# A twelve-stage transformer stack on one core: gate products taken batch by batch and weighed on GpSimd, six copies of parts in place of seven, the first half of the stacks fetched alone, and the mixtures' small arrays awaited later

## The chip, the core and the metric

The kernel runs on 1 core of one Trainium2 chip, in one launch. The metric is the device time in microseconds (us). Five engines work beside each other and meet only at semaphores: TensorE (PE, matmuls into the eight PSUM banks), VectorE (DVE), ScalarE (ACT), GpSimd (POOL) and SyncE (SP, which here only issues DMAs). ACT issues a few DMAs too, and POOL issues the indirect ones.

## What is computed

`x` is 4 x 512 x 128 float32: 4 batches of 512 tokens (16 tiles of 128 tokens) with 128 channels. Twelve sublayers are added to it one after the other, each on a layer-normed `x`:

```python
x = x + 0.5 * ffn0(ln(x));  x = x + gla(ln(x));            x = x + 0.5 * ffn0(ln(x))
x = x + 0.5 * moe1(ln(x));  x = x + attention1(ln(x));     x = x + 0.5 * moe1(ln(x))
x = x + 0.5 * moe2(ln(x));  x = x + diff_attention2(ln(x)); x = x + 0.5 * moe2(ln(x))
x = x + 0.5 * ffn3(ln(x));  x = x + diff_attention3(ln(x)); x = x + 0.5 * ffn3(ln(x))
```

Three kinds of sublayer matter here. The gated linear attention (`gla`) takes, beside q, k and v, three gates per head:

```python
h = x * rsqrt(mean(x * x) + 1e-06) * norm_w
def gate(W, b):                       # for Wbeta, Wig, Wog; 8 heads each, 24 columns in all
    return sigmoid(einsum('bld,hd->blh', h, W) + b)
```

The first mixture (`moe1`) sends each token to one of 8 experts, the second (`moe2`) to two:

```python
logits = einsum('bsh,he->bse', x, router_w) + router_b          # moe1
expert_idx = argmax(logits, axis=-1)
h = gelu(einsum('bsh,hi->bsi', x + 0.1 * game_emb[e], w1[e]) + b1[e])
y = einsum('bsi,ih->bsh', h, w2[e]) + b2[e]                      # of the token's expert e
```

The attentions take scores between heads of 8 or 4 channels (`attention1`: `softmax(y y^T / sqrt(8))`, 16 heads; the differential ones: two softmaxes per head, one subtracted from the other).

## The kernel before, in words

Each stage is one or two blocks. In a block every engine runs its own list of instructions; a new block begins on all engines once all have ended the last. The order on each engine is the order of the code; waits on semaphores are written out by hand. All tensors of tokens lie as 128 partitions x 16 tiles x 128.

**Norm.** `norm_rows` (L355 on) has DVE write the normed rows `N`, one TENSOR_SCALAR for each tile (L362): four of batch 0, then three of each later batch, whose last row ACT writes (L377). `norm_turn` has PE transpose the four tiles of a batch into one PSUM bank (L398), and ACT copies the bank to `nT` (L383, `norm_take`).

**The head of `gla`.** PE transposes all four batches into banks 0 to 3. Then it waits for `weighted` and takes 16 gate products `nT x WA[:, 384:408]` (L618, 128 x 24 each, every float32 matmul shown as two passes) into bank 0. `weighted` comes from DVE, which multiplies the 128 x 408 weights by `norm_w` (L655) behind its rows, three memsets (L649 to L651) and a cast of `FUT` (L653). POOL only casts `HR` (L607, L608). From the gates there is one chain over DVE, ACT and PE (L660 to L684) to the end of the block.

**The head of a mixture.** The router's products are already in a bank when the stage begins. SP issues the small arrays (L1117: `fixed`, `UPTO`; in `moe1` then `rbias`, `b1`, `b2` of 1 MB and `game`), then the stores of the normed rows, then the down weights (L1150), and after `EIDI` is known the first up weights (L1158). DVE scales the logits (L1348), waits for all small arrays (`dve.wait_ge(small.sem, ...)`, in front of L1352), adds the router's bias (`moe1`), finds the chosen expert (`best_of`, L1338 to L1342, twice in `moe2`) and scans them (L1360). `fixed` is first read at L1366 (COLS). POOL waits for the same small arrays and makes `UPTOB` (L1175), for which, and for the scan, PE's products of ranks wait (L1247 to L1249). Their result starts a long DVE chain (L1372 on) to the row numbers `ROWS`, with which POOL gathers the tokens of the first expert (L1180).

**The head of an attention.** A projection is split into three bfloat16 parts (high by ACT, mid by ACT, low by POOL) held in `PART`. SP copies them into `scratch` in HBM, where each side (0 for q, 1 for k) has six slots; `copies` says which part goes to which slots, one DMA for each entry (L1841 and L2341). Scores contract over the slots, so that slot n of q meets slot n of k. When all is written, stacks `QS` and `KM` or `KS` are fetched in two halves (h = 0, 1), for batch 0 the k side by ACT's queue (L2051, L2468), the rest by SP's (L1860, L2350). In the differential attentions half 1 of batch 0 waits for half 0 already; in `attention1` it does not. PE's first score waits for half 0.

## Time and profile before

| | |
|---|---|
| median of 3 runs | 1893.79 us (1889.36 to 1898.24) |
| the profiled execution | 1894.98 us, span of its engines 1893.2 us |
| PE busy | 1501.6 us (79%) |
| DVE busy | 1083.7 us (57%) |
| ACT busy | 938.9 us (50%) |
| POOL busy | 372.6 us (20%) |
| mean granted TensorE clock | 0.888 of full speed |

The busy shares are means over twelve stages with different limits. The places of this change are short stretches at the heads of stages, in which one engine after the other waits; there the order of time and the waits are read, not the shares. Granted clock 0.50 is 1.2 GHz, 1.00 is 2.4 GHz. The time outside the span is 1.8 us.

### The profile page before, as it was taken

The numbers are of one execution on the slowest core, as the hardware profiler recorded it, in microseconds if no ns is written. First come the engines' busy times: TensorE is split into PE (matmuls) and PEld (weight loads), VectorE is DVE, ScalarE is ACT, GpSimd is POOL, SyncE is SP. The second block draws the span as 40 slices with busy tenths as digits, with TensorE's granted clock in tenths as the row PEclk, the third lists the DMA queues.
The fourth block names the chain that finished last, engine by engine and source line by source line (L and its number), as shares of the span: only waits on it lengthen the run. The fifth ranks groups of instructions, "written<-read, shape, count | busy, mean of one in ns | idle before, by whom it ended". The sixth has DMA issues, their size and how long they took to land. (4 is left out here: it accounts for less than half of the span.)

```text
span 1893.2 us, 27972 instructions
## 1 busy us (share of the span) xinstructions
PE 1501.6 (79%) x9134; PEld 815.3 (43%) x9134; DVE 1083.7 (57%) x2375; ACT 938.9 (50%) x2167; POOL 372.6 (20%) x538
## 2 busy tenths in 40 slices
PE   4895757999999495883899999994883958999768
PEld 4354643555555383872222222223773532222345
DVE  6575431333334526215988898957214758878466
ACT  3454334445444253223687878783222236777522
POOL 0230530000000171771311010000671001110000
PEclk7796777999999796996899999996896978999979
DMA  2002534020200455554121111003453023330000
GB/s 71 5 1 62 172 116 114 5 67 1 67 1 1 127 153 170 158 140 116 44 58 43 37 44 35 1 1 101 136 151 119 0 77 88 78 79 1 1 1 22
DMA packets 96046, 126.01 MB, mean 67 GB/s; under 512 B 14612, under 2 KB 65684, under 8 KB 95404
## 3 DMA queue, kind: packets, MB, share of 16 engines
q1 hardware_dynamic: 86252, 105.19, 19.5%
q0 software_dynamic: 7936, 16.27, 3.3%
q10 hardware_dynamic: 1728, 2.88, 0.8%
q8 instruction: 74, 1.21, 0.3%
q14 instruction: 56, 0.46, 0.1%
HBM read 87.49 MB, written 36.80 MB: 66 GB/s over the span
## 5 line engine op out<-in xcount | busy, mean ns | idle before, releaser
L2090 DVE TENSOR_REDUCE MAXI<-psum 128x2 f32<-128x1024 f32 x384 | 457.0, 1219 | 91.2 <-PE psum L1897 88.6
L2007 ACT ACTIVATE EX<-psum 128x512 f32<-128x512 f32 x768 | 412.6, 605 | 107.0 <-PE psum L1918 106.9
L1918 PE MATMUL psum<-QM,KM 64*128 64x512 bf16 x768 | 227.4, 383 | 32.4 <-ACT EX L2007 21.6
L2389 PE MATMUL psum<-EX,N 128*128 128x512 f32 x512 | 238.6, 609 | 0.0
L2451 ACT ACTIVATE EX<-psum 128x512 f32<-128x512 f32 x256 | 149.3, 599 | 174.1 <-PE psum L2381 174.1
L1897 PE MATMUL psum<-KM,QS 64*128 64x512 bf16 x768 | 184.3, 401 | 35.9 <-DMA QS<-parts 20.8
L1928 PE MATMUL psum<-EX,VST 128*32 128x512 f32 x1536 | 203.1, 604 | 1.0 <-ACT OT L2021 1.0
L1214 PE MATMUL psum<-m_XT,m_W 128*128 128x128 f32 x992 | 144.5, 292 | 30.1 <-DVE m_XT L1438 24.0
L1445 DVE TENSOR_SCALAR m_Y<-psum 128x128 f32<-128x128 f32 x124 | 36.1, 291 | 219.6 <-DMA y<-m_Y,m_ROWS 141.6
L2500 DVE COPY OT<-psum 128x512 f32<-128x512 f32 x64 | 44.3, 692 | 187.1 <-PE psum L2389 187.1
L1918 PEld LDWEIGHTS psum<-QM,KM 64*128 64x128 bf16 x768 | 56.6, 94 | 217.5 <-ACT EX L2007 155.8
L1214 PEld LDWEIGHTS psum<-m_XT,m_W 128*128 128x128 f32 x992 | 128.6, 202 | 43.6 <-DVE m_XT L1438 33.5
L2389 PEld LDWEIGHTS psum<-EX,N 128*128 128x128 f32 x512 | 93.1, 191 | 119.7 <-issue 119.3
L1180 POOL DMA_INDIRECT m_XG<-rows,m_ROWS x124 | 122.0, 984 | 105.4 <-DVE m_ROWS L1407 68.8
L1309 ACT ACTIVATE m_H<-psum 128x512 f32<-128x512 f32 x78 | 46.6, 597 | 176.9 <-PE psum L1214 176.9
L1228 PE MATMUL psum<-m_DOWN,m_H 128*128 x992 | 133.3, 278 | 0.9 <-ACT m_H L1307 0.4
L1186 POOL DMA_INDIRECT y<-m_Y,m_ROWS x124 | 122.0, 984 | 42.6 <-issue 31.4
L1228 PEld LDWEIGHTS psum<-m_DOWN,m_H 128*128 128x128 f32 x992 | 123.2, 195 | 1.4 <-issue 1.2
L2184 POOL CAST NM<-MAXI 128x16 bf16<-128x16 f32 x48 | 12.2, 255 | 508.9 <-DVE MAXI L2090 508.9
L398 PE MATMUL psum<-ident,N 128*128 128x128 f32 x128 | 29.5, 393 | 91.2 <-DVE N L362 90.9
L1307 ACT ACTIVATE m_H<-psum,m_B 128x128 f32<-128x128 f32 x184 | 52.6, 368 | 81.7 <-PE psum L1214 80.1
L1897 PEld LDWEIGHTS psum<-KM,QS 64*128 64x128 bf16 x768 | 38.7, 94 | 121.2 <-issue 64.0
(319 smaller groups left out, 2129.3 us busy)
## 6 DMA issues: line engine op xcount, KB each, us to landing
m_W<-in_w_dram SPq DMA_DIRECT2D x124, 256.0 KB
parts<-PART SPq DMA_DIRECT2D x36, 256.0 KB, 2.4
m_DOWN<-in_w_dram SPq DMA_DIRECT2D x32, 256.0 KB, 4.6
parts<-PART SPq DMA_DIRECT2D x12, 384.0 KB, 2.6
parts<-PART SPq DMA_DIRECT2D x36, 128.0 KB, 2.1
rows<-N SPq DMA_DIRECT2D x16, 256.0 KB, 3.2
N<-y SPq DMA_DIRECT2D x16, 256.0 KB, 4.3
QS<-parts SPq DMA_DIRECT2D x32, 128.0 KB, 3.8
```

Source lines behind the costliest of these rows:

```text
L1180: pool.indirect_dma_start(XG[:, r % AHEAD, :], None, rows_dram, bass.IndirectOffsetOnAxis(ap=ROWS[:, 0, r:r + 1].bitcast(U32), axis=0)).th ...
L1186: pool.indirect_dma_start(y_dram, bass.IndirectOffsetOnAxis(ap=ROWS[:, 1, r:r + 1].bitcast(U32), axis=0), Y[:, r % 3, :], None).then_inc(s ...
L1214: last = pe.matmul(banks[2 + r % 2][:, it * P:(it + 1) * P], W[:, r % DEEP, it * P:(it + 1) * P], XT[:, r % 2, :], start=True, stop=True)
L1228: last = pe.matmul(banks[4 + r % 2][:, 0:P], H[:, r % 2, it * P:(it + 1) * P], DOWN[:, bass.ds(e, 1), it * P:(it + 1) * P].rearrange("p e ...
L1307: last = act.activation(H[:, r % 2, s], banks[2 + r % 2][:, s], ACT.Gelu, bias=B1[:, r, it:it + 1])
L1897: last = pe.matmul(pair(i)[:, k, :], QS[r, buf, g, qt * P:(qt + 1) * P], KM[r, buf, g, m, :], start=True, stop=True)
L1918: pe.matmul(bank_of(("score", n, i)), KM[r, buf, g, m, kt * P:(kt + 1) * P], QM[r, n % 2, MAPS[at] // slots, :], start=True, stop=True).th ...
L1928: last = pe.matmul(banks[4][32 * j:32 * j + 32, :], VST[:, n % 2, c, j // 2, :], EX[:, n % 2, c, j, :], start=c == 0 and n % GROUP == 0, s ...
L2007: act.activation(EX[:, n % 2, kt, MAPS[j], :], bank_of(("score", n, i)), ACT.Exp, scale=SM_SCALE).then_inc(S["exp"].sem, 1)
L2090: dve.tensor_reduce(MAXI[:, n % 2, qt, columns], pair(i), AX, ALU.max, negate=True).then_inc(S["reduced"].sem, 1)
L2389: last = pe.matmul(banks[4 + j], N[:, n // per_b * TB + kt, :], EX[:, n % 2, kt, j, :], start=kt == 0, stop=kt == TB - 1)
L2451: act.activation(EX[:, n % 2, kt, j, :], bank_of(("score", n, i)), ACT.Exp, scale=SM_SCALE, accum_out=SUMS[:, n % 2, j, kt:kt + 1]).then_i ...
```

## The change

1. `rbias`, the router's bias of `moe1` (4 KB), becomes a tensor of the whole kernel, loaded once by SP in the first block. Both `moe1` stages lose one small DMA.
2. In all four mixtures DVE's wait for the small arrays moves from in front of the choice of the experts to in front of COLS.
3. In `gla`, POOL multiplies the weights by `norm_w`, sets `M` and `VG` to zero and casts `FUT`; DVE loses these. PE takes the gate products by batch between the transposes, into bank 4.
4. `copies`: the k side has three DMAs for four, with other slots; the six pairs of parts that meet are the same.
5. In `attention1` half 1 of the stacks of batch 0 waits, on SP's and on ACT's queue, for half 0 (both sides).

```diff
@@ __init__
+        self.rbias = sb("rbias", [P, E])
@@ load
                 sp.dma_start(self.prefer[:], a["prefer"]).then_inc(consts.sem, 16)
+                sp.dma_start(self.rbias[:], a["rbias"]).then_inc(consts.sem, 16)
...
-                pe.wait_ge(consts.sem, 64)
+                pe.wait_ge(consts.sem, 80)
...
@@ gla, first block, gpsimd
                 pool.wait_ge(loaded.sem, 16 * len(arrays))
+                pool.tensor_scalar(WA[:], WA[:], NWC[:, 0:1], None, ALU.mult).then_inc(S["weighted"].sem, 1)
                 pool.tensor_copy(HRB[:].rearrange("r h t -> r (h t)"), HR[:]).then_inc(S["headrows"].sem, 1)
...
+                pool.memset(M[:], 0.0)
+                pool.memset(VG[:], 0.0)
+                pool.tensor_copy(FUTB[:], FUT[:])
@@ gla, first block, tensor
-                for b in range(B):
-                    self.norm_turn(pe, b)
+                self.norm_turn(pe, 0)
+                self.norm_turn(pe, 1)
                 pe.wait_ge(S["weighted"].sem, 1)
                 for t in range(NT):
-                    self.norm_ready(pe, t // TB)
-                    last = pe.matmul(banks[0][:, t * NG:(t + 1) * NG], nT[:, t * P:(t + 1) * P], WA[:, W3:W3 + NG],
+                    if t in (TB, 2 * TB):
+                        self.norm_turn(pe, t // TB + 1)
+                    if t % TB == 0:
+                        self.norm_ready(pe, t // TB)
+                    last = pe.matmul(banks[4][:, t * NG:(t + 1) * NG], nT[:, t * P:(t + 1) * P], WA[:, W3:W3 + NG],
                                      start=True, stop=True)
@@ gla, first block, vector
                 dve.memset(ONES[:], 1.0)
-                dve.memset(M[:], 0.0)
-                dve.memset(VG[:], 0.0)
                 dve.wait_ge(loaded.sem, 16 * len(arrays))
-                dve.tensor_copy(FUTB[:], FUT[:])
-                dve.tensor_scalar(WA[:], WA[:], NWC[:, 0:1], None, ALU.mult).then_inc(S["weighted"].sem, 1)
                 self.norm_rows_done(dve, B - 1)
@@ moe
-            rbias = sb("rbias", [P, E])
...
-            aux += [(rbias[:], "rbias"), (b1[:], "b1"), (b2[:], "b2"), (game[:], "game")]
+            aux += [(b1[:], "b1"), (b2[:], "b2"), (game[:], "game")]
...
-                dve.wait_ge(small.sem, small.at(16 * len(aux)))
                 if one:
-                    ch.link(dve.tensor_tensor(v, logits, rbias[:].unsqueeze(1).broadcast_to(s3), ALU.add))
+                    ch.link(dve.tensor_tensor(v, logits, self.rbias[:].unsqueeze(1).broadcast_to(s3), ALU.add))
...
+                dve.wait_ge(small.sem, small.at(16 * len(aux)))
                 dve.tensor_copy(COLS[:], const["cols"])
@@ diff_attention and attention1
-        copies = (((0, (0, 1, 2)), (1, (3, 4)), (2, (5,))), ((0, (0, 3)), (0, (5,)), (1, (1, 4)), (2, (2,))))
+        copies = (((0, (0, 1, 2)), (1, (3, 5)), (2, (4,))), ((0, (2, 3, 4)), (1, (1, 5)), (2, (0,))))
@@ attention1, sync
                             sp.wait_ge(S["score"].sem, at8("score", (b - 2) * per_b + 4 * h + 3, 7))
+                        if b == 0 and h == 1:
+                            sp.wait_ge(stacked[0].sem, stacked[0].at(16 * 2 * slots))
@@ attention1, scalar
                 for h in range(2):
+                    if h == 1:
+                        act.wait_ge(stacked[0].sem, stacked[0].at(16 * 2 * slots))
                     for j in range(slots):
```

How the rows stand on the engines. First PE in the head of `gla`: `g_gla_w` are the weights `WA`, L398 (L400 in the changed kernel) the transposes, L618 (L627) the gate products. Before, from the fourth batch's transposes on:

```order
L398 MATMUL psum<-ident,N 128x128 [waits norm_rows_act,norm_rows]
L398 MATMUL psum<-ident,N 128x128 x3
L618 MATMUL psum<-g_gla_w,nT 128x24 [waits norm_ready,gla_weighted]
L618 MATMUL psum<-g_gla_w,nT 128x24 [waits norm_ready] x15
L623 MATMUL psum<-g_LF,g_upto 128x128 [waits gla_logs]
```

And now, from the second batch's transposes on:

```order
L400 MATMUL psum<-ident,N 128x128 [waits norm_rows_act,norm_rows]
L400 MATMUL psum<-ident,N 128x128 x3
L627 MATMUL psum<-g_gla_w,nT 128x24 [waits norm_ready,gla_weighted]
L627 MATMUL psum<-g_gla_w,nT 128x24 x3
L400 MATMUL psum<-ident,N 128x128 [waits norm_rows_act,norm_rows]
L400 MATMUL psum<-ident,N 128x128 x3
L627 MATMUL psum<-g_gla_w,nT 128x24 [waits norm_ready]
L627 MATMUL psum<-g_gla_w,nT 128x24 x3
```

Two batches are transposed, then four products of one batch and four transposes of a later one alternate; the wait for the weights stands behind two batches in place of four.

POOL in the same block; the row of the branch is its end in the first piece. Before:

```order
L602 UNCONDITIONAL_BRANCH [waits barrier_Pool_Activation_PE_DVE_SP_gather]
L607 CAST g_HRB<-g_headrows 24x1024 [waits gla_load]
L608 CAST g_SEL<-g_headrows 24x128
L594 UNCONDITIONAL_BRANCH
L733 UNCONDITIONAL_BRANCH [waits barrier_Pool_Activation_PE_DVE_SP_gather]
```

And now:

```order
L609 TENSOR_SCALAR g_gla_w<-g_gla_w,g_gla_nw 128x408 [waits gla_load]
L610 CAST g_HRB<-g_headrows 24x1024
L611 CAST g_SEL<-g_headrows 24x128
L613 MEMSET g_M 128x512
L614 MEMSET g_VG 128x1024
L615 CAST g_FUTB<-g_future 128x512
```

The weighing stands at POOL's start, and three more instructions behind the two that were there.

DVE in the head of the first mixture; `stage_load` is the semaphore of the small arrays, `m_UPCOUNT` the scan, `m_COLS` the first reader of `fixed`. Before:

```order
L1348 TENSOR_TENSOR rt<-psum,rs 128x128 [waits route_scored]
L1352 TENSOR_TENSOR rt<-rt,m_rbias 128x128 [waits stage_load,route_step]
L1338 TENSOR_REDUCE m_CS<-rt 128x16 [waits route_step]
L1339 TENSOR_TENSOR rt<-rt,m_CS 128x128 [waits route_step]
L1340 TENSOR_TENSOR rt<-rt,prefer 128x128 [waits route_step]
L1341 TENSOR_REDUCE rt<-rt 128x16 [waits route_step]
L1342 TENSOR_TENSOR m_OH<-rt 128x16x8 [waits route_step]
L1360 SCALAR_TENSOR_TENSOR m_UPCOUNT<-m_RESET,m_OH 128x128 [waits moe_constants,route_step]
L1366 CAST m_COLS<-m_fixed 128x128
L1372 TENSOR_TENSOR m_GT<-psum,m_fixed 128x128 [waits moe_chosen,moe_ranked]
```

And now:

```order
L1351 TENSOR_TENSOR rt<-psum,rs 128x128 [waits route_scored]
L1354 TENSOR_TENSOR rt<-rt,rbias 128x128 [waits route_step]
L1341 TENSOR_REDUCE m_CS<-rt 128x16 [waits route_step]
L1342 TENSOR_TENSOR rt<-rt,m_CS 128x128 [waits route_step]
L1343 TENSOR_TENSOR rt<-rt,prefer 128x128 [waits route_step]
L1344 TENSOR_REDUCE rt<-rt 128x16 [waits route_step]
L1345 TENSOR_TENSOR m_OH<-rt 128x16x8 [waits route_step]
L1362 SCALAR_TENSOR_TENSOR m_UPCOUNT<-m_RESET,m_OH 128x128 [waits moe_constants,route_step]
L1369 CAST m_COLS<-m_fixed 128x128 [waits stage_load]
L1375 TENSOR_TENSOR m_GT<-psum,m_fixed 128x128 [waits moe_chosen,moe_ranked]
```

The wait on `stage_load` has passed seven instructions of DVE.

## Rows read from the trace of the kernel before

**Rows 1.** Waits: engine, line, releaser: us in total, times, longest.

```profile
DVE rt L1352 <- DMA m_game<-in_game_dram: 14.3, 2, 7.3
DVE m_CS L1338 <- DMA m_UPTO<-in_upto_dram: 3.3, 2, 1.6
SPq L1158 <- PE psum L1214: 157.8, 103, 12.7
```

**Rows 2.** Order of time, first mixture's head: start, us, engine, line, operation.

```profile
178.49 0.28 DVE L1348 TENSOR_TENSOR rt<-psum,rs 128x128 f32<-128x128 f32 x1
178.71 0.42 SPq L1117 DMA_DIRECT2D m_rbias<-in_rbias_dram  x1
179.17 0.91 SPq L1117 DMA_DIRECT2D m_b<-in_b_dram  x2
...
185.84 0.55 POOL L1175 TENSOR_SCALAR m_UPTOB<-m_UPTO 128x128 bf16<-128x128 f32 x1 [7.59 <-DMA m_game<-in_game_dram]
185.86 0.42 DVE L1352 TENSOR_TENSOR rt<-rt,m_rbias 128x128 f32<-128x128 f32 x1 [7.09 <-DMA m_game<-in_game_dram]
...
188.91 0.17 PE L1247 MATMUL psum<-m_UPCOUNT,m_ONESB 128*128 128x8 bf16 x1 [11.35 <-DVE m_UPCOUNT L1360]
...
189.35 0.29 DVE L1372 TENSOR_TENSOR m_GT<-psum,m_fixed 128x128 f32<-128x128 f32 x1 [0.47 <-PE psum L1249]
```

**Rows 3.** Order of time, head of the last `moe2`.

```profile
1308.35 0.28 DVE L1338 TENSOR_REDUCE m_CS<-rt 128x16 f32<-128x128 f32 x1 [1.63 <-DMA m_UPTO<-in_upto_dram]
```

**Rows 4.** Order of time, head of `gla`.

```profile
32.55 1.03 POOL L607 CAST g_HRB<-g_headrows 24x1024 bf16<-24x1024 f32 x1 [32.10 <-issue]
34.23 1.97 PE L398 MATMUL psum<-ident,N 128*128 128x128 f32 x8 [0.49 <-DVE N L362]
38.13 7.02 PE L618 MATMUL psum<-g_gla_w,nT 128*128 128x24 f32 x32 [0.55 <-DVE g_gla_w L655]
45.19 0.56 DVE L660 TENSOR_TENSOR g_Z<-psum,g_gla_gb 128x384 f32<-128x384 f32 x1 [4.91 <-PE psum L618]
```

**Rows 5.** Order of time, DVE alone, 32.4 to 32.7 us.

```profile
32.22 0.34 DVE L362 TENSOR_SCALAR N<-X,mv,rs 128x128 f32<-128x128 f32 x1
32.56 1.09 DVE L362 TENSOR_SCALAR N<-X,mv,rs 128x128 f32<-128x128 f32 x1
```

**Rows 6.** POOL's groups by shape: count, busy us, mean ns.

```profile
L742 POOL TENSOR_TENSOR g_QX<-g_QKT,g_quarter 128x512 f32<-128x512 f32 x16 | 16.6, 1039 | 54.1 <-ACT g_QKT L864 54.1
L1175 POOL TENSOR_SCALAR m_UPTOB<-m_UPTO 128x128 bf16<-128x128 f32 x4 | 2.2, 544 | 19.4 <-DMA m_game<-in_game_dram 15.3 <-DMA m_UPTO<-in_upto_dram 4.0
```

**Rows 7.** Stretches: length, busy us of PE, PEld, DVE, ACT, POOL, clock, DMA share, GB/s.

```profile
38.20:45.10 6.90, 6.90 (x32) 6.83 (x32) 2.08 (x1) 1.30 (x2) 0.00 (x0) 0.50 0.01 2
282.00:286.00 4.00, 0.00 (x0) 0.00 (x0) 0.00 (x0) 2.62 (x4) 1.16 (x1) 0.71 1.01 342
888.00:891.00 3.00, 0.76 (x7) 0.57 (x6) 2.27 (x2) 2.99 (x6) 0.00 (x0) 1.00 0.91 307
...
288.00:292.00 4.00, 0.00 (x0) 0.00 (x0) 0.00 (x0) 0.00 (x0) 0.00 (x0) 0.50 0.98 194
1552.00:1556.00 4.00, 0.00 (x0) 0.00 (x0) 0.00 (x0) 0.00 (x0) 0.00 (x0) 0.50 1.02 236
```

**Rows 8.** Order of time, head of `attention1`.

```profile
286.99 1.80 ACTq L2468 DMA_DIRECT2D KS<-parts  x4
293.62 1.04 PE L2381 MATMUL psum<-QS,KS 48*128 48x512 bf16 x4 [12.43 <-DMA KS<-parts]
294.24 0.60 ACT L2451 ACTIVATE EX<-psum 128x512 f32<-128x512 f32 x1 [9.60 <-PE psum L2381]
299.57 5.96 PE L2389 MATMUL psum<-EX,N 128*128 128x512 f32 x8
305.99 3.70 PE L2389 MATMUL psum<-EX,N 128*128 128x512 f32 x8
```

**Rows 9.** ACT's queue, last attention: the fetches of its second half.

```profile
1557.91 1.35 ACTq L2051 DMA_DIRECT2D KM<-parts  x2
```

More of the change, by code:

```diff
@@ L226, in _ @@
                     self.moments(dve, b)
-                dve.wait_ge(consts.sem, 64)
+                dve.wait_ge(consts.sem, 80)
                 dve.tensor_copy(self.identb[:], self.ident[:])
@@ L659, in _ @@
                 z, az, neg = Z[:, 0], Z[:, 1], Z[:, 2]
-                ch.link(dve.tensor_tensor(z, banks[0][:, 0:NT * NG].rearrange("p (t g) -> p t g", g=NG),
+                ch.link(dve.tensor_tensor(z, banks[4][:, 0:NT * NG].rearrange("p (t g) -> p t g", g=NG),
                                           GB[:].unsqueeze(1).broadcast_to([P, NT, NG]), ALU.add))
@@ L2276, in attention1 @@
         items = B * per_b
-        copies = (((0, (0, 1, 2)), (1, (3, 4)), (2, (5,))), ((0, (0, 3)), (0, (5,)), (1, (1, 4)), (2, (2,))))
+        copies = (((0, (0, 1, 2)), (1, (3, 5)), (2, (4,))), ((0, (2, 3, 4)), (1, (1, 5)), (2, (0,))))
         stage = ExitStack()
```

## The prediction, made before the changed kernel ran

> **What bounds the kernel now.** I read the waits grouped by engine first, then the order of time at the head of each stage that the change touches, then the stretches with clock and DMA rate, and POOL's groups by shape. All engines meet at the end of every stage, so a microsecond that a head loses is lost by all, and the busy shares of the page say little about it.
>
> In the waits the reader should look for an engine held by a DMA that it need not have waited for. DVE stands 14.3 us, twice about 7.1, in front of the router's bias of the two `moe1` stages, until the array `game` has landed [rows 1]. The order of time shows what that costs: the logits are scaled at 178.77, DVE goes on at 185.86, the scan ends just before 188.91, and only then can PE make the ranks with which the long chain at 189.35 starts [rows 2]. In the two `moe2` stages the same wait is 3.3 us in all, 1.63 in the one shown [rows 1, 3]. In the head of `gla`, PE waits for the weighing until 38.13 and then takes 16 gate products in 7.02 us; DVE can go on at 45.19 [rows 4]. In the head of `attention1`, PE waits for the stacks until 293.62 and ACT's first exponential starts at 294.24 [rows 8].
>
> **The mixtures' wait.** In `moe1` the choice and the scan (185.86 to 188.9, 3.05 us) move in front of the wait, which is 7.1 us long, so they are hidden whole. What is late next is not DVE but POOL: `UPTOB` waits for the same arrays, takes 0.55 us, and PE's ranks need it. So the ranks start at landing + 0.55 + about 0.1, and the chain 0.44 later, the distance from 188.91 to 189.35 [rows 2]. The arrays also land earlier: SP no longer issues `rbias` in front of `b1`, one step of 0.46 us (178.71 to 179.17), and `game`, which lands last, is behind it. That puts the landing at 185.84 - 0.46 = 185.38, the chain at 186.47, and the saving at 189.35 - 186.47 = 2.88. COLS now wakes on DVE together with `UPTOB` on POOL and may hold it a little; I take 2.8 for each, 5.6 for both. If the 1 MB of `b2` hides the shorter queue, it is 2.4 each. At most, a whole DMA more of 0.46 is won: 3.3 each.
>
> In `moe2` the wait of 1.63 goes entirely, since POOL's `UPTOB` (0.544 us [rows 6]) is done long before the second choice ends. It now falls beside DVE's choice. Beside POOL the bias add of `moe1` took 0.42 us, where the operation of the same shape ahead of it took 0.28 [rows 2], so I take 0.15 off: 1.48 each, 2.96. If POOL holds DVE for its whole 0.544, it is 1.1 each. The first `moe2` gathers while its weights still stream, which I charge with 0.1. So 2.9 for both, between 2.1 and 3.26.
>
> Behind these heads nothing is tied to a fixed time: SP waits 157.8 us for PE to free a weight buffer [rows 1], so the weights follow the tiles and not the other way, and the tile loops move forward whole. Mixtures: 5.6 + 2.9 - 0.1 (a first gather that begins while DVE still fills tables) = 8.4, bounds 6.9 and 9.9.
>
> **The head of `gla`.** PE's work from the second batch's transposes on is the same: 1.97 us for eight transposes is 0.88 for four with 0.2 of filling, three batches are 2.64; the gates are 7.02 [rows 4]. Together 9.66, now without a hole. If it starts at 34.23 as before, it ends at 43.9, 1.3 before 45.19. The hole before 38.13 is what goes; the gates themselves are at clock 0.50 throughout, 6.9 of 6.9 us [rows 7], that is 1.2 GHz, and I leave them there.
>
> Against this stands what POOL does to DVE. DVE's row at 32.56 took 1.09 us and the one ahead of it 0.34 [rows 5]; the only other thing that started at 32.55 is POOL's cast of 1.03 us [rows 4], and the long row ends 0.07 behind it. I read that as DVE held by POOL. Now POOL's weighing comes first, 128 x 408. No row shows it: at the 2.03 ns a column of L742 it is 0.83 us, in proportion to L1175 (0.544 for 128 columns) 1.73 [rows 6]. I take 1.0, near L742, because L1175's 128 columns must hold a large fixed part. Then the row at 32.56 ends at about 33.6, the next is held by the cast of 1.03 to 34.65, the third passes at 34.95, and PE's second batch starts at 35.0 instead of 34.23. 35.0 + 9.66 = 44.7: saving 0.5. With 1.73 the start is 35.7 and the result 0.2 later than before; with 0.83 and DVE passing between POOL's instructions it starts as before, and 1.3 is saved. The sets to zero and the cast of `FUT` end on POOL at about 37, by the 1.0 ns a column of its cast [rows 4]; their first reader stands in the next block, behind 45.19. DVE's addition of the bias to X moves ahead by 1.5 us and was hidden under the gates anyway.
>
> The Trainium skill has a rule for this, which speaks against the change: on the page "SBUF — State Buffer", section "Who interferes with whom", a VectorE instruction in a 2-port mode (tensor_scalar among them) and a GpSimd instruction share a pair of ports under an exclusive lock, and the second to issue "fully blocks until the first finishes". The trace agrees in the one place where it can be seen, 1.09 for 0.34 [rows 5]. By it DVE also holds POOL, and then neither order is safe; without the rule, with POOL's weighing beside DVE at no cost, the term would be 1.3 and not 0.5.
>
> **Six transfers for seven.** The bytes are the same. In `attention1` the copies run at 342 GB/s with the DMA engines full from 282 to 286 [rows 7], so one issue fewer is hidden by the queue: 0. In the differential heads the last copies stream at 307 GB/s, share 0.91, from 888 to 891 [rows 7]: the hole is 0.3 us, of which the longer DMA can fill half, 0.15 for each of two heads. Sum 0.3. Bounds: 0, and an issue step of 0.46 at each of three heads, 1.4. The copies of batches 1 to 3 run beside the scores.
>
> **Half of the stacks alone.** Half 0 is four fetches of 192 KB, 0.79 MB. With both halves in flight the engines moved 194 GB/s from 288 to 292; with one half alone, in the last attention, 236 [rows 7]. 4.05 us against 3.33: PE starts up to 0.7 earlier than 293.62. But ACT now wakes with PE and has two fetches to issue before its first exponential. They took 1.35 us in the last attention [rows 9], while the exponential came 0.62 behind PE [rows 8]; cost 0.73. I take 0, bounds 0.7 either way. SP waits too, with nothing behind it but the next batch. Half 1 starts at about 293 instead of 288 and is first read by the fifth item; one item takes 6.4 us (299.57 to 305.99 [rows 8]), so there are some 25 us for it.
>
> On the page "DMA: Bandwidth & Descriptors", section "Queues, rings and completion order", the Trainium skill says that each ring's descriptors are consumed in ring order. Then half 0 went first already, and this part would be only its cost, -0.7; that case lies inside the forecast's own range. The trace leaves it open: PE's wait ended 6.6 us after the first issue, where one half at 194 GB/s needs 4 [rows 7, 8].
>
> **The load.** One DMA more ahead of the routers, 0.46 us on SP. DVE is still at its moments then: 0, at worst 0.46 lost.
>
> **Sum.** 8.4 + 0.5 + 0.3 + 0 + 0 = 9.2 us. Against the profiled execution, 1894.98 us (span 1893.2 and 1.8 around it), that is 1885.8. This execution lies 1.2 above the median 1893.79; from the median, 1884.6. About 9.5 us, 0.5%, is what a measurement of this kernel tells from no change, so the forecast lies on that edge.
>
> **Rivals.** (1) POOL holds DVE longer. For it: the one stretched row [rows 5] and L1175's price [rows 6]. Against: L742's. `gla` loses 0.2, each `moe2` gives only 1.1: 9.2 - 0.7 - 0.8 = 7.7, time 1886.1. (2) The clock rises in the denser head of `gla`, where PE runs unbroken for 9.7 us. At 2.4 GHz half of the gates' 7.0 is 3.5 us less: 12.7, time 1881.1. Against: PE ran unbroken for 6.9 us of these products at 0.50 [rows 7]. (3) The mixtures give their gain back, because gathers and weights which begin earlier fall into the stream of down weights. For it: engines full in that stretch. Against: SP waits for PE, not PE for SP [rows 1]. With half given back the time is 1889. (4) Slower than before: the clock. In `attention1` the first item's value products took 5.96 us and the next 3.70 [rows 8], the price of the low clock, 2.26 an item. If PE, with ACT's start delayed, stays low for more items, each costs that; from the fifth on the whole gain is gone (4.1 x 2.26 = 9.2), and at nine items more the time is 1895. Against: ACT is late by tenths only.
>
> **Chances.** Forecast 0.58, (1) 0.22, (2) 0.06, (3) 0.09, (4) 0.05. Range: 1878.5, which holds the clock's case and a measurement that falls low, to 1890.5, which holds (3); the forecast's own is 1881 to 1888. Faster by over 0.5%: half of the forecast, somewhat less of (1), all of (2): 0.45. Within 0.5%: 0.50. Slower: 0.05.
>
> **What would show it.** Right: in both `moe1` heads COLS waits on `game`, and PE's ranks start 0.6 to 0.7 behind it; no DMA wait is left in the choice of `moe2`; the sum of idle time of DVE in front of the choices falls by 17.6 us, of which about 8.5 show in the span. In `gla` PE runs without a hole from 35.0 to 44.7, and L362 shows two stretched rows. Wrong: the ranks wait for something else, the tile loops of the mixtures become longer, the gates run at 1.00, ACT's first exponential in `attention1` is over 0.5 us late, or two executions differ by more than the sum.

## The result, and the profile after

| | before | after |
|---|---|---|
| median of 19 runs each | 1894.89 us (1889.36 to 1898.24) | 1885.66 us (1881.20 to 1890.22) |
| ratio | | 0.9952, 95% interval 0.9943 to 0.9960 |
| profiled execution, span | 1894.98, 1893.2 us | 1890.22, 1888.4 us |

The kernel got 9.2 us faster (7.6 to 10.8 by the interval), 0.48%, which is on the edge of the 0.5% that the forecast named. The forecast was 1884.6 us, and 9.2 us for the sum. The profiled execution of after is the slowest of its 19, so the two spans differ by 4.8 us only. Stages are therefore read from their own start; each opens with ACT's square root of the norm, and from one such start to the next it took, in us:

| | load, ffn0 | gla | ffn0 | moe1 | attention1 | moe1 | moe2 | diff 2 | moe2 | ffn3 | diff 3 | ffn3 |
|---|---|---|---|---|---|---|---|---|---|---|---|---|
| before | 30.9 | 123.5 | 23.5 | 96.6 | 360.1 | 97.8 | 144.2 | 429.2 | 142.7 | 86.8 | 270.3 | 87.6 |
| after | 30.3 | 121.9 | 23.8 | 92.0 | 362.4 | 97.2 | 142.7 | 428.8 | 143.5 | 87.7 | 270.7 | 87.4 |

`attention1` lost 2.3 us, and one has to know whether the change did that.

The waits of after that answer to [rows 1] (engine, line, releaser: us in total, times, longest):

```profile
DVE m_COLS L1369 <- DMA m_game<-in_game_dram: 7.9, 2, 4.1
POOL m_UPTOB L1178 <- DMA m_game<-in_game_dram: 14.6, 2, 7.5
```

The 14.3 us in front of the router's bias are gone, as are the 3.3 in front of the choice of `moe2`; 7.9 have come back in front of COLS. In the head of the first `moe1`, in order of time (start, us), to be held against [rows 2]:

```profile
176.61 0.28 DVE L1351 TENSOR_TENSOR rt<-psum,rs 128x128 f32<-128x128 f32 x1
...
179.28 0.42 DVE L1362 TENSOR_TENSOR_SCAN m_UPCOUNT<-m_RESET,m_OH 128x128 bf16<-128x128 bf16 x1
183.46 0.23 DVE L1369 CAST m_COLS<-m_fixed 128x128 bf16<-128x128 f32 x1 [3.76 <-DMA m_game<-in_game_dram]
183.52 0.57 POOL L1178 TENSOR_SCALAR m_UPTOB<-m_UPTO 128x128 bf16<-128x128 f32 x1 [7.14 <-DMA m_game<-in_game_dram]
184.14 0.19 PE L1250 MATMUL psum<-m_UPCOUNT,m_ONESB 128*128 128x8 bf16 x1 [8.46 <-POOL m_UPTOB L1178]
184.60 0.29 DVE L1375 TENSOR_TENSOR m_GT<-psum,m_fixed 128x128 f32<-128x128 f32 x1 [0.91 <-PE psum L1252]
```

The scan ends 3.1 us behind the start of the logits. `game` lands at 6.85 (before: 7.35), the ranks start 0.68 behind that, and the chain over DVE begins at 7.99 where it began at 10.86. Both engines then stand still for arrays that they do not need yet: COLS reads only `fixed`, and POOL's `UPTOB` only `UPTO`. In the last `moe2` nothing up to GT waits for a DMA any more; GT comes 6.3 us behind the logits, 1.6 sooner:

```profile
1306.01 0.29 DVE L1375 TENSOR_TENSOR m_GT<-psum,m_fixed 128x128 f32<-128x128 f32 x1 [0.39 <-PE psum L1252]
```

The head of `gla`, which answers to [rows 4, 5]; its first normed row is at 30.80 (before: 31.45):

```profile
32.03 1.55 POOL L609 TENSOR_SCALAR g_gla_w<-g_gla_w,g_gla_nw 128x408 f32<-128x408 f32 x1 [31.57 <-issue]
33.54 1.14 POOL L610 CAST g_HRB<-g_headrows 24x1024 bf16<-24x1024 f32 x1
34.64 0.35 POOL L611 CAST g_SEL<-g_headrows 24x128 bf16<-24x128 f32 x1
34.94 0.52 POOL L613 MEMSET g_M<- 128x512 f32 x1
35.41 1.16 POOL L614 MEMSET g_VG<- 128x1024 f32 x1
```

```profile
30.80 0.34 DVE L364 TENSOR_SCALAR N<-X,mv,rs 128x128 f32<-128x128 f32 x1
31.91 4.80 DVE L364 TENSOR_SCALAR N<-X,mv,rs 128x128 f32<-128x128 f32 x9
33.65 1.90 DVE L364 TENSOR_SCALAR N<-X,mv,rs 128x128 f32<-128x128 f32 x1
35.53 1.12 DVE L364 TENSOR_SCALAR N<-X,mv,rs 128x128 f32<-128x128 f32 x1
...
42.48 0.56 DVE L664 TENSOR_TENSOR g_Z<-psum,g_gla_gb 128x384 f32<-128x384 f32 x1 [3.16 <-PE psum L627]
```

```profile
33.18 0.47 PE L400 MATMUL psum<-ident,N 128*128 128x128 f32 x1
```

The line x9 is all nine rows behind the fourth (3.14 us before), the two below it are the longest of them. The prediction named two stretched rows; here two last over 1 us, and not those that I named: they stand beside POOL's casts and sets. Beside its weighing one row takes 0.70 and the first, where I expected 1.0, 0.34. The record of a row can overlap that of the next: inside the 1.90 us of one row the next one begins (at 34.69). PE turns the second batch at 33.18, 2.38 behind the first row, works without a hole, and DVE goes on 11.68 us behind that row (before 13.74).

The head of `attention1` ([rows 8] before; its opening square root is at 268.05, before at 274.55):

```profile
287.10 0.84 ACTq L2475 DMA_DIRECT2D KS<-parts  x2
287.21 1.04 PE L2386 MATMUL psum<-QS,KS 48*128 48x512 bf16 x4 [11.78 <-DMA KS<-parts]
287.98 0.60 ACT L2456 ACTIVATE EX<-psum 128x512 f32<-128x512 f32 x1 [9.83 <-PE psum L2386]
293.30 6.60 PE L2394 MATMUL psum<-EX,N 128*128 128x512 f32 x8
```

The first exponential comes 0.77 behind the first score (before 0.62), and the first item's value products take 6.60 us (before 5.96).

### The profile page after: what moved, and what is told of

Same layout as the page of the kernel before. It is cut to its first block and busy times, and to the rows that moved or that the text cites. A ratio compares the mean times of both kernels' runs of the same rounds, so it can differ in the third digit from the quotient of the medians.

```text
span 1888.4 us, 27953 instructions
## 1 busy us (share of the span) xinstructions
PE 1504.0 (80%) x9134; PEld 815.3 (43%) x9134; DVE 1084.3 (57%) x2371; ACT 939.2 (50%) x2167; POOL 375.7 (20%) x542
## 5 line engine op out<-in xcount | busy, mean ns | idle before, releaser
L1921 PE MATMUL psum<-QM,KM 64*128 64x512 bf16 x768 | 227.7, 386 | 31.7 <-ACT EX L2010 21.3
L400 PE MATMUL psum<-ident,N 128*128 128x128 f32 x128 | 30.2, 398 | 91.0 <-DVE N L364 90.9
```

Of the source, the lines that this page charges most:

```text
L1921: pe.matmul(bank_of(("score", n, i)), KM[r, buf, g, m, kt * P:(kt + 1) * P], QM[r, n % 2, MAPS[at] // slots, :], start=True, stop=True).th ...
```

## The experiments

Except where it is said, a variant is the kernel before with one piece. They ran on three other chips, one after the other, on each of which the kernel before takes 1963 to 1965 us: its mixtures are 11 to 24 us longer there, the other stages as above. So every ratio is to the kernel before as measured beside it on the same chip, and stage lengths of mixtures are compared among these three chips only. I tell heads by distances from a row of the same stage.

**The mixtures alone.**

```diff
-                dve.wait_ge(small.sem, small.at(16 * len(aux)))
                 if one:
-                    ch.link(dve.tensor_tensor(v, logits, rbias[:]...
+                    ch.link(dve.tensor_tensor(v, logits, self.rbias[:]...
...
+                dve.wait_ge(small.sem, small.at(16 * len(aux)))
                 dve.tensor_copy(COLS[:], const["cols"])
```

> The kernel before with the mixtures' part alone. Theory (the wait is hidden behind the choice): in both moe1 heads the first operation on the ranks comes 2.7 to 2.9 us sooner after the scaled logits, in both moe2 heads 1.5 to 1.6 sooner, the tile loops behind them are as long as before, and the time falls by 8.4 us (ratio 0.9956). Rival (the loops give half back): the heads gain the same, but from the first gather to the end of the stage each mixture takes about 1 us longer, and the time falls by 4 to 5 us. This kernel has gla, the copies and the stacks as before, so gla's head stays at 13.7 us from the first normed row to the gates' first reader and attention1's clock rises as before, 29.7 us into the stage.

Measured: ratio 0.9955 (0.9939 to 0.9970), 8.8 us. Every later profile shows the four heads as well, so they can be averaged. From the scaled logits to the first product with up weights, in us:

| | old head (7 profiles) | new head | gain |
|---|---|---|---|
| first `moe1` | 26.61 (26.39 to 26.85) | 23.64 (23.47 to 23.71), 4 profiles | 2.97 |
| second `moe1` | 26.76 (26.49 to 26.96) | 24.11 (23.82 to 24.71), 4 | 2.65 |
| first `moe2` | 28.22 (28.10 to 28.72) | 27.41 (27.16 to 27.78), 7 | 0.81 |
| second `moe2` | 28.20 (28.14 to 28.25) | 26.60 (26.53 to 26.68), 7 | 1.60 |

Together 8.0 us. From there to the end of the stage it took, on the three other chips, 81.4, 85.7, 136.4 and 135.5 us with the old heads and 81.3, 85.9, 134.7 and 135.1 with the new: the loops give nothing back, and the rival falls. (On the first chip the one profile of each kernel has 369.4 us for the four before and 371.5 after: the first `moe1` is 1.7 and the first `moe2` 0.6 shorter, the second ones 2.1 and 2.4 longer. The other chips, with three to six profiles of each, do not repeat it.)

The first `moe2` keeps only 0.81 of the 1.58 that it has at GT. Between the gather and the first up product the engines still carry weights. These are stretches from 2 to 4 us behind the first gather, of before (gather at 756.98) and of after (750.62), in the form of [rows 7]:

```profile
759.00:761.00 2.00, 0.58 (x2) 0.29 (x3) 0.29 (x1) 0.00 (x0) 1.39 (x3) 0.50 0.14 39
```

```profile
752.60:754.60 2.00, 0.21 (x1) 0.18 (x1) 0.00 (x0) 0.00 (x0) 1.39 (x3) 0.50 0.75 257
```

The DMA share is 0.14 before and 0.75 after. That fits the reason that the prediction gave for its 0.1, but no run moves the weights to test it.

**The head of gla alone**, both pieces: POOL weighs, sets and casts, PE takes the gates batch by batch.

```diff
+                pool.tensor_scalar(WA[:], WA[:], NWC[:, 0:1], None, ALU.mult).then_inc(S["weighted"].sem, 1)
                 pool.tensor_copy(HRB[:].rearrange("r h t -> r (h t)"), HR[:]).then_inc(S["headrows"].sem, 1)
...
+                    if t in (TB, 2 * TB):
+                        self.norm_turn(pe, t // TB + 1)
```

> The kernel before with the gla part alone (weighing, sets to zero and casts on POOL, gate products batch by batch). Theory formed from the profile of the changed kernel: from the first normed row to the first reader of the gates it takes 11.7 us where it took 13.74, because the weighing of 1.55 us leaves DVE nearly free; the saving is 2.0 us and all of it reaches the end of the stage: time 2.0 less, ratio 0.9989. Rival (the forecast's mechanism): the weighing holds DVE, the second batch's transposes start 3.5 us behind the first row, and the saving is 0.5 us. A second rival: the head gains 2.0 but something later in gla gives it back, so the whole stage stays at 123.5 us.

Measured: ratio 0.9991 (0.9980 to 1.0003), first row to the gates' reader 11.69 us, the stage 121.8 us. The head gains 2.06 and the stage 1.7 (123.1 to 123.5 in four profiles with the old head): the part behind the gates' reader is 0.4 longer. The interval of the ratio holds no change too; what shows the gain is the distance in the head, 11.68 or 11.69 us in seven profiles with both pieces and 13.74 or 13.75 in four without either.

**PE's order alone, and POOL's part alone.** The first leaves the weighing with DVE, the second leaves PE's order.

```diff
-                for b in range(B):
-                    self.norm_turn(pe, b)
+                self.norm_turn(pe, 0)
+                self.norm_turn(pe, 1)
                 pe.wait_ge(S["weighted"].sem, 1)
```

```diff
+                pool.tensor_scalar(WA[:], WA[:], NWC[:, 0:1], None, ALU.mult).then_inc(S["weighted"].sem, 1)
...
-                dve.tensor_scalar(WA[:], WA[:], NWC[:, 0:1], None, ALU.mult).then_inc(S["weighted"].sem, 1)
```

> The kernel before with PE's new order alone: two batches turned, then the wait for the weighing, which DVE makes behind its rows, sets and cast as before. Theory: PE is held from the second batch's turn until 6.7 us behind the first row, and then has two batches to turn and 16 products to take, 1.8 + 7.0: first reader at 15.5 us, 1.8 later than in the kernel before. Rival (the order alone brings the gain): 11.7 to 12.5.

> The kernel before with the weighing, the sets and the cast on POOL, but with PE's old order (four batches turned, then 16 gate products into bank 0). Theory (order and engine are worth something only together): DVE's rows end 5.9 us behind the first one as in the changed kernel, PE has turned the last batch at about 6.8, takes 7.0 for the gates, and their first reader comes at 13.8, as in the kernel before (13.74). Rival (the engine alone brings the gain): 11.7 to 12.5.

Measured (one profile each; first rows at 30.61 and 30.86): the gates' reader 15.24 and 13.77 us behind the first row. Neither piece brings anything alone; the order alone costs 1.5.

```profile
45.85 0.56 DVE L663 TENSOR_TENSOR g_Z<-psum,g_gla_gb 128x384 f32<-128x384 f32 x1 [6.41 <-PE psum L621]
```

```profile
44.63 0.56 DVE L659 TENSOR_TENSOR g_Z<-psum,g_gla_gb 128x384 f32<-128x384 f32 x1 [5.26 <-PE psum L622]
```

**The casts and sets ahead of the weighing.**

```diff
                 pool.tensor_copy(FUTB[:], FUT[:])
+                pool.tensor_scalar(WA[:], WA[:], NWC[:, 0:1], None, ALU.mult).then_inc(S["weighted"].sem, 1)
```

> The kernel before with the gla part alone, but with POOL's casts and sets to zero ahead of its weighing. Theory: POOL's casts and sets take 3.8 us by the changed kernel's rows, so the weighing ends 6.5 us behind the first row; PE has turned two batches by then and has 8.8 us left, so the gates' reader comes at 15.3 us, 1.6 later than in the kernel before and 3.6 later than in the changed kernel. DVE's rows at the casts are stretched as in the kernel before: one of 1.1 us at HRB. Rival (it is the batch-wise order on PE that brings the gain and not who weighs, or when): the reader comes at 11.7 to 12.5.

Measured: 14.37 us; slower than before, but by 0.6 and not by 1.6, as the casts and sets took 3.3 us and not 3.8. On DVE the row beside them was not 1.1 long but 2.69; the last line below is this row together with the next. These are that kernel's POOL and DVE in order of time:

```profile
32.46 1.03 POOL L607 CAST g_HRB<-g_headrows 24x1024 bf16<-24x1024 f32 x1 [32.01 <-issue]
33.44 0.28 POOL L608 CAST g_SEL<-g_headrows 24x128 bf16<-24x128 f32 x1
33.67 0.51 POOL L610 MEMSET g_M<- 128x512 f32 x1
34.13 0.94 POOL L611 MEMSET g_VG<- 128x1024 f32 x1
```

```profile
32.47 2.69 DVE L362 TENSOR_SCALAR N<-X,mv,rs 128x128 f32<-128x128 f32 x1
32.47 2.76 DVE L362 TENSOR_SCALAR N<-X,mv,rs 128x128 f32<-128x128 f32 x2
```

One row of 0.34 us ends only behind four POOL instructions, at 35.16. The next begins at 33.49, when the first cast ends, as in the kernel before, and ends 0.07 behind it; the third row begins at 35.15, 1.4 later than before. So it is the two sets (0.51 and 0.94 us) that delay the rows beyond what the cast did already. PE's second batch is turned at 35.82 for that reason.

**Three more weighings.** The changed kernel, with useless work behind the weighing:

```diff
+                for k, dst in enumerate((flat[:, 0:408], flat[:, 408:816], flat[:, 0:408])):   # flat: VG
+                    pool.tensor_scalar(dst, WA[:], NWC[:, 0:1], None, ALU.mult).then_inc(spare.sem, 1)
+                    pool.wait_ge(spare.sem, k + 1)
```

> The changed kernel with three more weighings (the same operation, 128 x 408, into the place of VG, before that is set to zero) between POOL's weighing and its casts: work that is of no use, added to see what it does to DVE. Theory (POOL's weighing leaves DVE nearly free, its casts and sets to zero hold it): DVE's nine normed rows behind the fourth take 3 us instead of 4.8, no row over 0.7 us while the weighings run, and the gates' first reader stays at 11.7 us behind the first row, since PE sets it. Rival (a 128-partition operation on POOL holds a VectorE row as long as it lasts): each weighing holds a row for 1.5 us, the nine rows take 6 us or more, PE's last two batches start later and the gates' reader comes at 13 us or later.

Measured: the gates' reader at 11.68, DVE's nine rows in 3.3 us (4.8 in the changed kernel). POOL, and DVE's nine rows with the longest of them:

```profile
32.58 1.55 POOL L609 TENSOR_SCALAR g_gla_w<-g_gla_w,g_gla_nw 128x408 f32<-128x408 f32 x1 [32.12 <-issue]
34.23 1.38 POOL L614 TENSOR_SCALAR g_VG<-g_gla_w,g_gla_nw 128x408 f32<-128x408 f32 x1
...
37.10 2.52 POOL L614 TENSOR_SCALAR g_VG<-g_gla_w,g_gla_nw 128x408 f32<-128x408 f32 x1
```

```profile
32.47 3.29 DVE L364 TENSOR_SCALAR N<-X,mv,rs 128x128 f32<-128x128 f32 x9
34.20 0.71 DVE L364 TENSOR_SCALAR N<-X,mv,rs 128x128 f32<-128x128 f32 x1
```

Beside weighings some rows take 0.7 and others 0.34, none waits for a weighing's end. The weighing is not free: the first four rows follow each other at 0.26 us, by which nine would take 2.4, so the nine that ran beside weighings lost 0.9 together, about 0.3 for each us of weighing. But POOL's casts and sets hold a row for as long as they last, and the weighing does not: that is shown by this pair of kernels. What makes the difference (the operation, the types, the 24 partitions of the casts) was not tested.

**Six transfers for seven.**

```diff
-        copies = (((0, (0, 1, 2)), (1, (3, 4)), (2, (5,))), ((0, (0, 3)), (0, (5,)), (1, (1, 4)), (2, (2,))))
+        copies = (((0, (0, 1, 2)), (1, (3, 5)), (2, (4,))), ((0, (2, 3, 4)), (1, (1, 5)), (2, (0,))))
```

> The kernel before with six transfers of parts for seven alone. Theory: nothing in attention1 (its first score stays at 19.1 us behind the square root that opens the stage), 0.15 us in each differential head, 0.3 in all, ratio 0.9998. Rival (an issue step of SP is on the path): 0.46 us at each of the three heads, first scores sooner by that, 1.4 us in all, ratio 0.9993. A third: the two DMAs of three slots each on one side run at another rate than 307 to 342 GB/s, and a head moves by more than 0.5 us either way.

Measured: ratio 1.0002 (0.9988 to 1.0015). In `attention1` the first score is at 19.20 (19.07 before, and 19.07 to 19.46 in the seven profiles with the old order of the halves). In the differential heads it scatters by more than the term: over seven profiles with seven transfers 21.1 to 23.0 (mean 22.15) and 21.6 to 23.0 (22.13), over seven with six 21.3 to 22.5 (22.03) and 21.0 to 22.7 (22.02). 0.1 each is no measurable gain; none above 0.5 is there.

**The first half of the stacks alone.**

```diff
+                        if b == 0 and h == 1:
+                            sp.wait_ge(stacked[0].sem, stacked[0].at(16 * 2 * slots))
...
+                    if h == 1:
+                        act.wait_ge(stacked[0].sem, stacked[0].at(16 * 2 * slots))
```

> The kernel before with the first half of attention1's stacks fetched alone. Theory formed from the profile of the changed kernel (the engines served the first half first already): PE's first score stays at 19.1 us behind the opening square root, ACT's first exponential comes 0.2 later, the granted clock rises 0.9 us later than before (30.6 us into the stage), and the stage gets 0.9 us longer, ratio 1.0005. Rival (the halves shared the engines): the first score comes up to 0.7 us sooner, and the stage is as long as before or up to 0.7 shorter. If the later rise of the clock in the changed kernel was chance, it rises here at 29.7 as before.

Measured: ratio 1.0003 (0.9990 to 1.0016), `attention1` 359.5 us and not 361, the clock up at 28.6 us into the stage. My theory of the loss, a later rise of the clock, was wrong. The head:

```profile
307.78 1.04 PE L2383 MATMUL psum<-QS,KS 48*128 48x512 bf16 x4 [11.51 <-DMA KS<-parts]
308.55 0.60 ACT L2453 ACTIVATE EX<-psum 128x512 f32<-128x512 f32 x1 [9.60 <-PE psum L2383]
```

The first score is at 18.92 and the exponential at 19.69. Over seven profiles each: score at 19.24 without and 18.99 with the change, exponential at 19.86 and 19.76.

**The changed kernel again**, on one of the other chips.

> The changed kernel itself, on the chip on which its variants run. Theory (heads save 8.0 to 8.5 in the mixtures and 1.7 in gla; what attention1 lost in the first profile was chance): ratio 0.995, attention1 between 359.5 and 361 us, its first item's value products between 5.4 and 6.6 us wherever the clock happens to rise. Rival (fetching the first half alone keeps the clock low longer): attention1 at 362 us again.

Measured: ratio 0.9962 (0.9949 to 0.9974), `attention1` 359.5 us, its first value products 5.13 us, below the 5.4 that I expected at least. These products took 5.0 to 6.6 us in the seven profiles without the half alone and 5.1 to 6.6 in the seven with it: only where the clock rises, 28 to 31 us into the stage, decides, and it does so alike in both kinds. From the second item's value products to the last item's, all fourteen profiles take the same time, 317.05 to 317.06 us. The other 1.4 us of the 2.3 are at the end. Stretches of the first profile of after and of this one (length, busy us of PE, PEld, DVE, ACT, POOL, clock, DMA share, GB/s):

```profile
624.40:627.40 3.00, 3.00 (x28) 3.00 (x27) 1.56 (x13) 1.16 (x3) 0.00 (x0) 0.91 0.00 0
627.40:630.40 3.00, 2.69 (x13) 2.59 (x13) 0.00 (x0) 0.16 (x2) 0.03 (x1) 0.50 0.00 0
```

```profile
636.90:639.90 3.00, 2.04 (x19) 1.95 (x17) 0.37 (x3) 0.81 (x2) 0.41 (x3) 0.86 0.00 0
```

The last products of the stage ran at clock 0.50 in the first and at 1.00 until the last of them in the second. Of the other twelve profiles one shows such a drop (362.2 us, the kernel with three more weighings), eleven do not (359.3 to 360.9). Both profiles with the drop fetch the first half alone, so it is two of seven with that piece and none of seven without: too few to tell chance from a small cost.

**A version that is faster than both.** Nothing of `b1`, `b2` and `game` is needed for the ranks. In the changed kernel:

```diff
+            for dst, name in later:                      # b1, b2, game
+                sp.dma_start(dst, a[name]).then_inc(late.sem, 16)
...
                     is_of = AFTER[:, 1]
+                    dve.wait_ge(late.sem, late.at(16 * len(later)))
...
                         pe.wait_ge(S["chosen_t"].sem, S["chosen_t"].at(2))
+                        pe.wait_ge(late.sem, late.at(16 * len(later)))
```

> The changed kernel, with b1, b2 and game on a semaphore of their own, which DVE awaits in front of the table of game rows and PE in front of the first product with b2; COLS and UPTOB wait for fixed and UPTO only. Theory (in moe1 the ranks waited for arrays that they don't read): the wait of 4 us in front of COLS goes, and the first operation on the ranks comes 3.7 us behind the logits instead of 8.0 to 8.3, as the choice and the scan take 3.1 and the products of the ranks 0.6. The gather and the first up product come 4.4 us sooner too, twice, so 8.8 less than the changed kernel: ratio to the kernel before 0.991. Rival (transfers are late next): the stored rows, 2 MB of down weights and the first up weights stand behind b2's 1 MB, so the gather or the first up product stays where it is: ranks 4.4 sooner, first up product at most 2 sooner, time like the changed kernel's or up to 4 less, ratio 0.9935 to 0.9955.

> The kernel of the early ranks again, beside the one with b2 moved. If its gain was real: ratio 0.989 to 0.992 to the kernel before, ranks 3.7 us behind the logits, first up product at 20.3 to 21.0. If it was the luck of one call: 0.993 or more.

Measured: 0.9904 (0.9889 to 0.9920), and in a second measurement 0.9905 (0.9890 to 0.9921): by these ratios 18.8 and 18.7 us faster than the kernel before, and in the first one 1944.97 us against 1954.82 for the changed kernel on the same chip, 10 us less (11 by the ratios). In order of time, first `moe1`:

```profile
174.12 0.28 DVE L1355 TENSOR_TENSOR rt<-psum,rs 128x128 f32<-128x128 f32 x1
175.89 0.54 POOL L1181 TENSOR_SCALAR m_UPTOB<-m_UPTO 128x128 bf16<-128x128 f32 x1 [2.00 <-DMA m_UPTO<-in_upto_dram]
177.36 0.17 PE L1254 MATMUL psum<-m_UPCOUNT,m_ONESB 128*128 128x8 bf16 x1 [4.17 <-DVE m_UPCOUNT L1366]
177.80 0.29 DVE L1379 TENSOR_TENSOR m_GT<-psum,m_fixed 128x128 f32<-128x128 f32 x1 [0.47 <-PE psum L1256]
```

The ranks now wait for the scan, and GT comes 3.68 us behind the logits. The gather is 4.3 to 5.4 us sooner, the first up product 3.4 and 3.8 sooner in the first measurement: from gather to up it takes 6.2 to 6.9 us instead of 5.2 to 5.3. So the heads account for 7 of the 10 us; where the rest comes from, chance included, no run shows. A likely reason for the slower gather is that the DMA engines are full while it runs. These are the 4 us behind its start in the first `moe1`, with early ranks (start at 188.26) and in the changed kernel (193.50) on the same chip:

```profile
188.30:192.30 4.00, 0.00 (x0) 0.00 (x0) 2.49 (x4) 0.00 (x0) 3.40 (x3) 0.50 0.98 340
```

```profile
193.50:197.50 4.00, 0.18 (x1) 0.18 (x1) 2.53 (x4) 0.00 (x0) 3.40 (x3) 0.50 0.13 40
```

The DMA share is 0.98 in one and 0.13 in the other.

**b2 behind the first up weights.** To win that back:

```diff
+                    if one and r == DEEP:
+                        sp.dma_start(b2[:], a["b2"]).then_inc(last_in.sem, 16)
                     if r >= DEEP:
                         sp.wait_ge(S["up"].sem, S["up"].at(r - DEEP + 1))
```

> The kernel of the early ranks, with b2 (1 MB, first read at the end of the stage) issued behind the first five up weights and no longer behind b1. Theory (the gathered rows come late because b2, the stored rows and the down weights fill the engines): the ranks stay at 3.7 us behind the logits and the gather at 14.1, and from the gather to the first up product it takes 5.2 to 5.6 us in the moe1 stages instead of 6.2 and 6.9, so 2 us less than the kernel of the early ranks in all. Rival (b2 only moves the load into the tile loop, which on this chip is held by transfers): the head gains 1 us per stage, the loop is 1 us longer, time as the kernel of the early ranks within 1 us. Second rival: it is the down weights that delay the gather, and nothing changes from gather to up.

Measured: 0.9925 (0.9908 to 0.9942), and 6.7 and 8.3 us from the gather to the up product. A miss: the head gains nothing in the first `moe1` (6.7 us with early ranks beside it too) and loses in the second. The intervals of the two ratios overlap, so that it is slower as a whole is not shown. What the trace shows is that 1 MB is now issued just when the first gathered rows are on their way. The second `moe1`, of this kernel and then of the one with early ranks:

```profile
654.46 0.34 SPq L1166 DMA_DIRECT2D m_b<-in_b_dram  x1
657.36 0.47 PE L1217 MATMUL psum<-ident,m_XG 128*128 128x128 f32 x1 [8.16 <-issue]
659.35 1.91 PE L1225 MATMUL psum<-m_XT,m_W 128*128 128x128 f32 x8
```

```profile
657.33 0.48 PE L1212 MATMUL psum<-ident,m_XG 128*128 128x128 f32 x1 [7.44 <-DMA m_XG<-rows,m_ROWS]
658.47 1.91 PE L1220 MATMUL psum<-m_XT,m_W 128*128 128x128 f32 x8
```

Their stages start at 636.4 and 637.1, so the rows come 0.7 later here and the up product 1.6.

## Why the prediction was right, and where a size was off

- **Mixtures, `moe1`: 5.6 forecast, 5.6 measured** (2.97 + 2.65). The mechanism is the one named: POOL's `UPTOB` is late next, the ranks start 0.68 behind the landing, and the shorter queue brings the landing 0.5 forward.
- **Mixtures, `moe2`: 2.9 less 0.1 forecast, 2.4 measured.** Up to GT each gained 1.58 (1.48 forecast). The first one pays 0.8 between the gather and the first up product (4.25 us in the mean of seven profiles, 5.03 in seven), not 0.1: of the terms of this part it is the one that was mis-sized. The second keeps all.
- **The head of `gla`: 0.5 forecast, 2.06 measured, outside the bounds of -0.2 to 1.3.** The step that failed is the transfer of "DVE held by POOL" from the cast of [rows 5] to the weighing. The weighing took 1.55 us, within 0.83 to 1.73 and above the 1.0 that I took, yet beside it no row lasted longer than 0.71; and the cast that holds DVE now came behind the second batch's rows. So that batch was turned 2.38 us behind the first row, 0.4 sooner than before, where I had it 0.8 later. PE's unbroken work was 9.3 us, not 9.66. Of the 2.06 the end of the stage keeps 1.7. In the rule of the Trainium skill, page "SBUF — State Buffer", section "Who interferes with whom", it is an exclusive lock for a whole instruction with whichever POOL instruction (the words quoted in the prediction stand in that page's section "Summary: rules for kernel authors"). The casts and sets behave so (a row ended only behind four of them, after 2.69 us), the weighings do not (no row over 0.71 beside 1.3 to 1.55 us), and the measurement decides.
- **Six transfers for seven: 0.3 forecast, not measurable** (0.1 at each differential head in a scatter of 2 us).
- **Half of the stacks alone: 0 forecast, 0 to 0.1 measured.** The two sides are smaller than forecast, 0.25 sooner for PE and 0.15 later for ACT behind it, not 0.7 and 0.73: the two issues of ACT took 0.84 us, most of it beside PE's first products. The Trainium skill, page "DMA: Bandwidth & Descriptors", section "Queues, rings and completion order", says that a ring's descriptors are consumed in ring order; from that the prediction concluded that the first half went first already. The runs agree in that it gained only 0.25 from being alone; ACT's cost of 0.7 did not come with it. A cost at the end of the stage (the drop of the clock in two of seven profiles) stays open.
- **The load: 0 forecast.** To the start of `gla` it took 29.4 to 30.9 us without the new DMA (mean of seven 30.3) and 29.7 to 31.2 with it (30.6): no difference that stands out of the scatter.
- **Sum.** 8.0 + 2.1 + 0.1 = 10.2 by the heads; the time says 9.2 (7.6 to 10.8). The forecast's 9.2 came about by 1.6 too little in `gla` against 0.4 too much in `moe2` and 0.3 not seen in the transfers. The mechanism of the mixtures, the greater part, was right; that the sum meets the measured 9.2 to a tenth is luck, as the heads have 1.0 more than forecast. That difference lies within the interval of the time.
- **Rivals.** (1), POOL holds DVE longer, falls as a loss of time: `gla` gained, and `moe2` gained 1.58 up to GT. DVE was held longer (nine rows in 4.8 us, not 3.14), but behind the rows that PE waited for first. (2), the clock in `gla`'s denser head: the gates stayed at 0.50, but see below. (3) falls by the loops' lengths, and (4) by `attention1` at 359.5 us in the second profile of the changed kernel. In (4) a sum is wrong: nine items at 2.26 would be 20 us and 1905, not 1895.

## What to carry to other kernels

Before a wait for a group of small arrays is moved, list for each waiting instruction which of the arrays it reads: here the moved wait brought 8 us, and splitting it some 10 us more, 7 of them seen in the heads. An order for PE and the engine that feeds it are one edit: each half of the `gla` head alone brought nothing or lost 1.5 us. When a term rests on one stretched row, ask what instruction stood beside it, because the next kind of instruction need not do the same.

## What the hardware showed beyond that

- One DVE row of 0.34 us ended only behind four POOL instructions in a row, casts and sets (2.69 us), and behind three in the changed kernel (1.90), though the row behind it had begun by then. POOL in turn took 2.52 us for a weighing beside DVE's addition of 2048 columns (L667, 2.45 us), 1.38 beside normed rows.
- `gla` has two lengths with the new head: 121.8 to 122.2 us in four profiles, 119.3 to 119.4 in three, the same kernel among both. In the short ones the granted clock rises 6 us sooner. These are two stretches, of after and of the changed kernel on the other chip:

```profile
66.00:72.00 6.00, 6.00 (x37) 2.77 (x39) 2.18 (x6) 3.38 (x13) 1.74 (x3) 0.50 0.00 0
```

```profile
67.00:73.00 6.00, 6.00 (x48) 2.73 (x47) 2.97 (x8) 3.47 (x14) 1.74 (x3) 0.83 0.00 0
```

  None of seven profiles with another head has the early rise. Whether the denser head makes it possible, or seven are too few, stays open; it would be worth 2.5 us where it happens. The heads of the short and the long ones are the same to 0.01 us, so the 2.06 of the head do not hang on it.
- The same program is 3.6 to 3.7% slower on three other chips than on the first, nearly all of it in the four mixtures, whose loops gather, scatter and stream weights.
